# Three small edits to an eight-core attention and feed-forward kernel: the matmuls at its start go, a ring of product buffers gets a fourth slot, a pair of hidden-layer buffers becomes one

## The chip, the cores and the metric

The kernel runs on the 8 cores of one Trainium2 chip (two dies of four cores). Every core works on its own two sequences of the batch of 16 and never talks to the others. The metric is the device time in microseconds of the slowest core. PE is TensorE, DVE is VectorE, ACT is ScalarE, POOL is GpSimd, SP is SyncE, which here issues the loads of x and the stores of y.

## The reference

One pre-norm transformer layer on x of 16 x 2048 x 1024 in f32:

```python
x = x + attn(layernorm(x), W_qkv, b_qkv, W_proj, b_proj)     # 16 heads of 64
x = x + ffn(layernorm(x), Win, bin_, W1, b1, W2, b2, Wout, bout)

# attn: softmax(q k^T / 8) v with a "Fenwick" mask: token i sees itself, i-1, i-2, i-4, ... i-1024
#       and those few j with i on the Fenwick path of j
# ffn:
s = einsum('btd,dm->btm', x, Win) + bin_          # 1024 -> 64
h = relu(s[..., None] * W1 + b1)                  # 64 x 16 hidden values a token
g = einsum('btmh,mh->btm', h, W2) + b2            # 64
out = einsum('btm,md->btd', g, Wout) + bout       # 64 -> 1024
```

## The kernel before

A core goes through 16 chunks of 256 tokens (CH), eight for each of its two sequences. Every instruction is emitted once in Python order into a queue for its engine (class `Prog`). An engine runs its queue strictly in that order, and an instruction waits for the semaphores that its `deps` name. So the order of emission sets what stands behind a waiting instruction.

At the start DVE clears buffers, POOL and SP issue the weight loads, and PE runs 256 matmuls on `ones32` (L273 to L276, recorded as L274), each 128 columns wide. Nothing reads what they write.

A chunk does its attention within its own 128-token blocks (scores L907 and L913 on PE, exponentials L920 on ACT, weighted values L837), the far keys (below), the projection (L981) and the second layer norm. Then it prepares the next chunk: q, k (L720) and v (L774, evacuated at L785), and at last the feed-forward stage of its own tokens, into which the far scores of the next chunk are woven.

The far scores are elementwise products. For each distance o of 256, 512 and 1024 that the next chunk reaches, and each of 8 blocks dc of channels, `build_sparse` makes one **step** (L594 to L631). Step number k forms q times shifted k in two halves of 64 partitions: the low half at L617, on POOL where dc is even and on DVE where it is odd; the high half at L619, always on DVE. Then one matmul (L623, called m(k) here) sums the product over channels. The products of step k lie in a ring slot. Slot 1 is the second half of `tmpsp`, the others are in `ebuf`. Before step k may write its slot, the matmul that read the slot last must be done (`ebuf_rd[es]`); with three slots that is m(k-3). A chunk whose successor is the first of a sequence, or that has none, weaves in no steps (chunks 7 and 15); two weave in 8 steps (0 and 8), four weave in 16 (1, 2, 9, 10) and eight weave in 24.

The feed-forward stage: `s_sTb` is made by L1041 and evacuated by ACT at L1044. The 1024 hidden values a token are done in 8 pieces, ic = 0 to 7. For piece ic, h(ic) is a matmul L1068 on PE; its relu e(ic) writes `hT`, on ACT for even ic (L1087) and on DVE for odd ic (L1091); g(ic) is a matmul L1099 on PE that reads `hT` and accumulates into one bank. Three h are emitted ahead, h(ic+3) reuses the bank that e(ic) has read. `hT` has two halves, so e(ic) waits for g(ic-2) (`hT_rd[hs]`). The order of emission:

```python
h(0); step; h(1); step; h(2); step          # L1073 to L1076
for ic in range(8):                         # L1078
    e(ic); h(ic+3) if ic+3 < 8; g(ic); step; step
gaugT (ACT, L1104); the steps that are left; exp of the far scores (L645),
their transposes (L661, L665); Wout matmuls (L1121); residual (L1127)
```

So PE meets h(ic+3) behind the two step matmuls of the round before, and DVE meets e(odd) behind the products of two rounds. The Wout matmuls stand on PE behind L661, and so behind the last step.

Of the kernel before, what the change touches and what calls it, by code (L numbers as in the profile page):

```python
# [7 lines left out]
BF16 = mybir.dt.bfloat16  # L8
# [167 lines left out]
def build_program(cfg):  # L176
    nc = bass.Bass("TRN2", target_bir_lowering=False)
    T, CH, BPC, C, H = cfg.T, cfg.CH, cfg.BPC, cfg.C, cfg.H
# [28 lines left out]
    sbt = lambda n, shp, dt: st.enter_context(nc.sbuf_tensor(n, shp, dt))  # L207
    pst = lambda n, shp, dt: st.enter_context(nc.psum_tensor(n, shp, dt))

    with st:  # L210
# [17 lines left out]
        ones32 = sbt("s_ones32", [32, 128], BF16)  # L228
# [10 lines left out]
        scb = sbt("s_scb", [16, NO * CH], F32)  # L239
        sct = sbt("s_sct", [128, TPC * NO * 16], BF16)  # L240
        tmpsp = sbt("s_tmpsp", [128, 2 * VA_W], BF16)
        ebuf = sbt("s_ebuf", [128, 2 * CH], BF16)
        oT = sbt("s_oT", [128, NDC * CH], BF16)
        sTb = sbt("s_sTb", [64, CH], BF16)
        gaugT = sbt("s_gaugT", [65, CH], BF16)
        hT = sbt("s_hT", [128, 2 * CH], BF16)
        stats = sbt("s_stats", [128, 16 * TPC], F32)
        recip16 = sbt("s_recip", [128, 16], F32)

# [14 lines left out]
        P = Prog()  # L264
# [4 lines left out]
        t_cst = [t_cexp, t_ceps, t_czer]  # L269
        t_o32a = P.emit("vector", lambda ec: ec.memset(ones32[:, :], 0.0))  # L270
        t_ones = P.emit("vector", lambda ec: ec.memset(ones32[0:1, :], 1.0), deps=[t_o32a])
        t_heat = t_ones
        for _hk in range(256):  # L273
            t_heat = P.emit("tensor", lambda ec: ec.matmul(  # L274
                psc[0][:, 0:128], ones32[0:32, 0:128], ones32[0:32, 0:128],
                start=True, stop=True), deps=[t_ones] if _hk == 0 else [])  # L276
        t_qz0 = P.emit("vector", lambda ec: ec.memset(qZ[:, :], 0.0))
        t_bvz = P.emit("vector", lambda ec: ec.memset(bv_row[:, :], 0.0))
        t_bpz = P.emit("vector", lambda ec: ec.memset(bproj_row[:, :], 0.0))
# [2 lines left out]
        for dc in range(NDC):  # L282
            for k in range(2):
# [3 lines left out]
                              deps=[t_bo0])  # L287
# [103 lines left out]
        xT_rd = [[], []]  # L391
        xln_rd = [[], []]
        xln_w = [[], []]
        ebuf_rd = [[], [], []]
        scr_rd = []
        tt1_rd = [[]]
        hT_rd = [[], []]
        pmask_rd = [[], [], [], []]
        praw_rd = [[], []]
        x_ring_free = [[], []]  # L400
# [170 lines left out]
        def build_sparse(c2, qz_done2, qkv_done2):  # L571
            t0s = c2 * CH
            tile0s = t0s // 128
            sct_ready2 = {}
            steps = []
            valid_big = [(oi, o) for oi, o in enumerate(BIG) if t0s + CH > o]
            if not valid_big:
                return steps, None, sct_ready2
            per_bank = max(512 // CH, 1)
            nbank = (len(valid_big) + per_bank - 1) // per_bank  # L580
            sc_banks = [SPB[k] for k in range(nbank)]
            st_cell = {"war": None, "final": None}

            def get_war():
                if st_cell["war"] is None:
                    w = []
                    for bk in sc_banks:
                        w += psc_readers[bk]
                    st_cell["war"] = w
                return st_cell["war"]  # L590

            ei_cell = [0]
            for vi, (oi, o) in enumerate(valid_big):
                scp = rotb[sc_banks[vi // per_bank]]  # L594
                col0 = (vi % per_bank) * CH
                a = max(0, o - t0s)
                w = CH - a
                for dc in range(NDC):
                    def step(vi=vi, oi=oi, o=o, dc=dc, scp=scp, col0=col0, a=a, w=w):
                        es = ei_cell[0] % 3  # L600
                        ei_cell[0] += 1
                        kap_lo = kT[0:64, dc * T + t0s + a - o: dc * T + t0s + a - o + w]
                        kap_hi = kT[64:128, dc * T + t0s + a - o: dc * T + t0s + a - o + w]
                        qlo = qZ[0:64, dc * CH + a: dc * CH + a + w]
                        qhi = qZ[64:128, NDC * CH + dc * CH + a: NDC * CH + dc * CH + a + w]
                        if es != 1:
                            e0 = (es // 2) * CH
                            elo = ebuf[0:64, e0 + a:e0 + a + w]
                            ehi = ebuf[64:128, e0 + a:e0 + a + w]
                            e_in = ebuf[:, e0 + a:e0 + a + w]  # L610
                        else:
                            elo = tmpsp[0:64, VA_W + a: VA_W + a + w]
                            ehi = tmpsp[64:128, VA_W + a: VA_W + a + w]
                            e_in = tmpsp[:, VA_W + a: VA_W + a + w]
                        dq = qz_done2.get(dc, qkv_done2)
                        lo_eng = "gpsimd" if dc % 2 == 0 else "vector"
                        t_e1 = P.emit(lo_eng, lambda ec, elo=elo, qlo=qlo, kap_lo=kap_lo: ec.tensor_mul(  # L617
                            elo, qlo, kap_lo), deps=dq + ebuf_rd[es] + (scr_rd if es == 1 else []))
                        t_e2 = P.emit("vector", lambda ec, ehi=ehi, qhi=qhi, kap_hi=kap_hi: ec.tensor_mul(  # L619
                            ehi, qhi, kap_hi), deps=dq + ebuf_rd[es] + (scr_rd if es == 1 else []))  # L620
                        boap = bo[:, dc * 16:(dc + 1) * 16]
                        out_ap = scp[0:16, col0 + a: col0 + a + w]
                        t_mm = P.emit("tensor", lambda ec, out_ap=out_ap, boap=boap, e_in=e_in, dc=dc: ec.matmul(  # L623
                            out_ap, boap, e_in, start=(dc == 0), stop=(dc == NDC - 1)),
                            deps=([t_e1, t_e2, t_bo] + get_war()) if dc == 0 else [t_e1, t_e2])
                        ebuf_rd[es] = [t_mm]
                        st_cell["final"] = t_mm
                        for jt in range((t0s + a - o) // 128, (t0s + a - o + w + 127) // 128):
                            kv_rd[jt].append(t_e1)
                            kv_rd[jt].append(t_e2)  # L630
                        qT_rd.append(t_e1)  # L631
                        qT_rd.append(t_e2)
                    steps.append(step)

            def finish():
                nonlocal scb_rd, sct_rd
                t_exp_by_oi = {}
                for vi, (oi, o) in enumerate(valid_big):
                    scp = rotb[sc_banks[vi // per_bank]]
                    col0 = (vi % per_bank) * CH  # L640
                    a = max(0, o - t0s)
                    w = CH - a
                    in_ap = scp[0:16, col0 + a: col0 + a + w]
                    out_ap = scb[0:16, oi * CH + a: oi * CH + a + w]
                    t_exp = P.emit("scalar", lambda ec, in_ap=in_ap, out_ap=out_ap: ec.activation(  # L645
                        out_ap, in_ap, AF.Exp, bias=-8.0, scale=0.125),
                        deps=[st_cell["final"]] + t_cst + scb_rd)
                    t_exp_by_oi[oi] = t_exp
                for bk in sc_banks:
                    psc_readers[bk] = list(t_exp_by_oi.values())  # L650
                for i in range(TPC):
                    qg = tile0s + i
                    for oi, o in valid_big:
                        if qg * 128 < o:
                            continue
                        bank = rot6_next()
                        dst = rotb[bank]
                        src_ap = scb[0:16, oi * CH + i * 128: oi * CH + (i + 1) * 128]
                        out_ap = sct[:, (i * NO + oi) * 16:(i * NO + oi) * 16 + 16]
                        idap = identf[0:16, 0:16]  # L660
                        t_tr = P.emit("tensor", lambda ec, dst=dst, src_ap=src_ap, idap=idap: ec.transpose(  # L661
                            dst[:, 0:16], src_ap, idap),
                            deps=[t_exp_by_oi[oi], t_identf] + psc_readers[bank])
                        scb_rd = [t_tr]
                        t_ev = P.emit("vector", lambda ec, dst=dst, out_ap=out_ap: ec.tensor_copy(  # L665
                            out_ap, dst[:, 0:16]), deps=[t_tr] + sct_rd)
                        psc_readers[bank] = [t_ev]
                        sct_ready2[(i, oi)] = t_ev

            return steps, finish, sct_ready2  # L670
# [17 lines left out]
        for idx, (b, c) in enumerate(sched):  # L688
# [391 lines left out]
            for ic in range(8):  # L1080
                bank = h_banks[ic]
                scp = rotb[bank]
                hs = ic % 2
                bap = b1col[:, ic:ic + 1]
                hout = hT[:, hs * CH:(hs + 1) * CH]
                if ic % 2 == 0:
                    t_hev = P.emit("scalar", lambda ec, hout=hout, scp=scp, bap=bap: ec.activation(  # L1087
                        hout, scp[:, 0:CH], AF.Relu, bias=bap, scale=1.0),
# [6 lines left out]
                if ic + NHB < 8:  # L1095
                    sTb_rd = [emit_hmm(ic + NHB, [t_hev], bank=bank)]
                lhs2 = w2exp[:, ic * 64:(ic + 1) * 64]
                hin = hT[:, hs * CH:(hs + 1) * CH]
                t_g_last = P.emit("tensor", lambda ec, pbG=pbG, lhs2=lhs2, hin=hin, ic=ic: ec.matmul(  # L1099
                    pbG[0:64, 0:CH], lhs2, hin, start=(ic == 0), stop=(ic == 7)),  # L1100
                    deps=[t_hev] + (pbr_get(biG) if ic == 0 else []))
# [121 lines left out]
```

How the kernel before makes its waits and increments, by code:

```python
    def replay(self, eng, ec, sems):  # L155
        for fn, waits, key, inc in self.q[eng]:
            for (sk, sv) in waits:
                ec.wait_ge(sems[sk], sv)
            if fn is not None:
                instr = fn(ec)
                if key is not None:
                    instr.then_inc(sems[key], inc)
```

## Time and profile before

| | us |
|---|---|
| two timed runs | 1405.37 and 1471.52 (median 1438.44) |
| the profiled execution | 1403.41 |
| its span, slowest core (core 5) | 1401.8 |
| spans of the eight cores | 1394.8 to 1401.8 |
| busy on that core: PE, DVE, ACT, POOL | 1124.6, 764.9, 402.0, 186.8 |

The span runs from the first to the last instruction of a core, and 1.6 us of the profiled execution lie around it. Times in the rows are microseconds from the start of the span. A row of the timeline gives start, duration, engine, line, operation, tiles and count (rows of one kind are merged), and in brackets how long the engine had stood idle before it and what released it. A PE row's duration includes the drain of the last matmul, so a matmul's duration is longer than the distance to the next one.

### The profile page before, as it was taken

The numbers are of one execution on the slowest core, as the hardware profiler recorded it, in microseconds if no ns is written. First come the engines' busy times: TensorE is split into PE (matmuls) and PEld (weight loads), VectorE is DVE, ScalarE is ACT, GpSimd is POOL, SyncE is SP. The second block draws the span as 40 slices with busy tenths as digits, with TensorE's granted clock in tenths as the row PEclk, the third lists the DMA queues.
The fourth block names the chain that finished last, engine by engine and source line by source line (L and its number), as shares of the span: only waits on it lengthen the run. The fifth ranks groups of instructions, "written<-read, shape, count | busy, mean of one in ns | idle before, by whom it ended". The sixth has DMA issues, their size and how long they took to land.

```text
span 1401.8 us, 22118 instructions; the slowest of 8 cores (1394.8 to 1401.8 us)
## 1 busy us (share of the span) xinstructions
PE 1124.6 (80%) x6912; PEld 643.5 (46%) x6912; DVE 764.9 (55%) x2080; ACT 402.0 (29%) x899; POOL 186.8 (13%) x193
## 2 busy tenths in 40 slices
PE   7078888898888877888888788888787887987885
PEld 7054545453534535335354544445353443534542
DVE  6055535546574565745654545555556565565654
ACT  0114132423313233132332424132422314223221
POOL 1000101102021030210300010100103012031130
PEclk9999889898978969789798989889897887878976
DMA  9900010101001010010101010010101001010000
GB/s 146 167 1 1 1 61 1 61 1 61 1 14 48 1 61 1 1 61 1 61 1 61 1 44 18 1 61 1 61 1 51 11 1 61 1 48 13 1 31 30
DMA packets 13279, 43.82 MB, mean 31 GB/s; under 512 B 2608, under 2 KB 2864, under 8 KB 13168
## 3 DMA queue, kind: packets, MB, share of 16 engines
q1 hardware_dynamic: 9584, 33.65, 6.9%
q0 software_dynamic: 3584, 8.76, 4.1%
q8 instruction: 61, 1.00, 0.3%
q14 instruction: 50, 0.41, 0.1%
HBM read 34.38 MB, written 16.78 MB: 36 GB/s over the span
## 4 chain that ended last, share of the span: by engine, by line
PE 57%; DVE 15%; issue 13%; ACT 6%; another core or an unknown queue 3%; DMA 2%; POOL 1%; DVEq 1%; POOLq 0%; ACTq 0%; SPq 0%
PE p_o L720 7%; PE p_o L774 6%; PE p_A L981 6%; PE p_A L720 4%; PE p_B L981 4%; PE p_o L494 3%; PE p_o L623 3%; PE p_B L720 3%; ACT s_pmask L920 2%; PE p_B L774 2%; PE p_sc L907 2%; DVE s_xT L502 2%; PE p_sc L913 2%; PE p_o L939 2%
## 5 line engine op out<-in xcount | busy, mean ns | idle before, releaser
L617 POOL TENSOR_TENSOR s_ebuf<-s_qZ,s_kT 64x256 bf16<-64x256 bf16 x94 | 63.2, 673 | 593.8 <-DVE s_qZ L731 542.6
L720 PE MATMUL p_o<-s_xT,s_wqkv 128*128 128x256 bf16 x1152 | 133.7, 273 | 0.0
L920 ACT ACTIVATE s_pmask<-p_sc 128x512 bf16<-128x512 f32 (+1 forms) x192 | 103.9, 591 | 86.4 <-PE p_sc L913 85.1
L720 PEld LDWEIGHTS p_o<-s_xT,s_wqkv 128*128 128x128 bf16 x1152 | 112.8, 98 | 13.2
L437 ACT ACTIVATE s_xln<-s_x 128x1024 f32<-128x1024 f32 x32 | 33.5, 1049 | 245.4 <-DVE s_stats L434 245.4
L981 PE MATMUL p_A<-s_wproj,s_oT 128*128 128x512 bf16 x256 | 89.5, 513 | 11.7 <-DVE s_oT L502 11.2
L720 PE MATMUL p_A<-s_xT,s_wqkv 128*128 128x256 bf16 x512 | 69.3, 274 | 34.2 <-DVE s_qZ L731 20.3
L494 PE MATMUL p_o<-s_identf,s_xln 128*128 128x128 f32 x376 | 76.6, 303 | 20.5 <-DVE s_recip L953 16.5
L837 PE MATMUL p_o<-s_vaug,s_pmask 128*128 128x66 bf16 x992 | 70.1, 196 | 28.5 <-ACT s_pmask L920 27.4
L774 PE MATMUL p_o<-s_wqkv,s_xT 128*128 128x512 bf16 x384 | 91.2, 380 | 0.0
L837 PEld LDWEIGHTS p_o<-s_vaug,s_pmask 128*128 128x128 bf16 x992 | 58.2, 100 | 62.2 <-issue 42.2
L907 PE MATMUL p_sc<-s_qZ,s_kT 128*128 128x256 bf16 x372 | 85.0, 314 | 0.0
L913 PE MATMUL p_sc<-s_mb,s_ident 128*128 128x512 bf16 (+1 forms) x192 | 83.6, 436 | 0.0
L623 PE MATMUL p_o<-s_ebuf,s_bo 128*16 128x256 bf16 x182 | 59.4, 346 | 18.7 <-DVE s_ebuf L619 18.0
L992 DVE SCALAR_TENSOR_TENSOR s_x<-p_A,s_x 128x512 f32<-128x512 f32 x32 | 22.1, 692 | 95.4 <-PE p_A L985 95.4
L866 POOL TENSOR_TENSOR s_tmpsp<-s_vaug,s_sct 128x1056 bf16<-128x1056 bf16 x28 | 54.6, 1949 | 138.7 <-DVE s_sct L665 56.1
L494 PE MATMUL p_sc<-s_identf,s_xln 128*128 128x128 f32 x131 | 32.2, 301 | 49.8 <-DVE s_stats L547 48.1
L617 POOL TENSOR_TENSOR s_tmpsp<-s_qZ,s_kT 64x256 bf16<-64x256 bf16 x42 | 27.9, 665 | 329.4 <-PE p_o L623 328.3
L785 DVE CAST s_vaug<-p_o 128x512 bf16<-128x512 f32 x48 | 33.3, 694 | 69.9 <-PE p_o L778 69.9
L720 PEld LDWEIGHTS p_A<-s_xT,s_wqkv 128*128 128x128 bf16 x512 | 48.1, 98 | 49.6 <-issue 44.2
L494 PEld LDWEIGHTS p_o<-s_identf,s_xln 128*128 128x128 f32 x376 | 49.5, 153 | 36.4 <-issue 35.6
L619 DVE TENSOR_TENSOR s_ebuf<-s_qZ,s_kT 64x256 bf16<-64x256 bf16 x182 | 64.5, 369 | 1.6 <-PE p_o L623 0.2
(153 smaller groups left out, 2013.7 us busy)
## 6 DMA issues: line engine op xcount, KB each, us to landing
s_x<-x SPq DMA_DIRECT2D x16, 1024.0 KB, 5.3
y<-s_x SPq DMA_DIRECT2D x16, 1024.0 KB, 4.4
s_wqkv<-wqkv POOLq DMA_DIRECT2D x1, 6144.0 KB, 50.9
s_wproj<-wproj POOLq DMA_DIRECT2D x1, 2048.0 KB, 61.6
s_win<-win POOLq DMA_DIRECT2D x1, 128.0 KB, 61.5
s_woutaug<-wout POOLq DMA_DIRECT2D x1, 128.0 KB, 57.0
s_identf<-ident SPq DMA_DIRECT2D x1, 64.0 KB, 1.8
s_mb<-mb01x POOLq DMA_DIRECT2D x1, 64.0 KB, 57.0
```

The costliest lines, as they stand in the source:

```text
L494: t_tr = P.emit("tensor", lambda ec, dst=dst, si=si, src_ap=src_ap: ec.transpose(dst[:, si * 128:(si + 1) * 128], src_ap, identf[:, :]), d ...
L617: t_e1 = P.emit(lo_eng, lambda ec, elo=elo, qlo=qlo, kap_lo=kap_lo: ec.tensor_mul(elo, qlo, kap_lo), deps=dq + ebuf_rd[es] + (scr_rd if es ...
L619: t_e2 = P.emit("vector", lambda ec, ehi=ehi, qhi=qhi, kap_hi=kap_hi: ec.tensor_mul(ehi, qhi, kap_hi), deps=dq + ebuf_rd[es] + (scr_rd if ...
L623: t_mm = P.emit("tensor", lambda ec, out_ap=out_ap, boap=boap, e_in=e_in, dc=dc: ec.matmul(out_ap, boap, e_in, start=(dc == 0), stop=(dc = ...
L720: t_mm = P.emit("tensor", lambda ec, pb=pb, lhs=lhs, rhs=rhs, dc=dc: ec.matmul(pb[:, 0:CH], lhs, rhs, start=(dc == 0), stop=(dc == NDC - 1 ...
L774: t_mm = P.emit("tensor", lambda ec, pb=pb, lhs=lhs, rhs=rhs, dc=dc: ec.matmul(pb[:, 0:512], lhs, rhs, start=(dc == 0), stop=False), deps= ...
L837: t_pv = P.emit("tensor", lambda ec, out_ap=out_ap, lhs=lhs, rhs=rhs, st=st, stp=stp: ec.matmul(out_ap, lhs, rhs, start=st, stop=stp), dep ...
L866: t_ttA = P.emit("gpsimd", lambda ec, tout=tout, vin=vin, prep=prep: ec.tensor_mul(tout, vin, prep), deps=[sct_ready[(i, oi)], t_va1] + tt ...
L907: t_last = P.emit("tensor", lambda ec, out_ap=out_ap, lhs=lhs, rhs=rhs, first=first: ec.matmul(out_ap, lhs, rhs, start=first, stop=False), ...
L913: t_last = P.emit("tensor", lambda ec, scp=scp, width2=width2, mrep=mrep: ec.matmul(scp[:, 0:width2], ident[:, :], mrep, start=False, stop ...
L920: t_exp = P.emit("scalar", lambda ec, pm=pm, scp=scp, width2=width2: ec.activation(pm, scp[:, 0:width2], AF.Exp, bias=-8.0, scale=0.125), ...
L981: t_mm = P.emit("tensor", lambda ec, pb=pb, lhs=lhs, rhs=rhs, dc=dc: ec.matmul(pb[:, 0:512], lhs, rhs, start=(dc == 0), stop=False), deps= ...
```

## The change

The 256 matmuls at the start are not emitted. The ring of the steps has four slots: slot 1 is still in `tmpsp`, slots 0, 2 and 3 are in `ebuf`, which grows from 512 to 768 columns. `hT` shrinks from 512 to 256 columns and all eight pieces use it.

```diff
-        ebuf = sbt("s_ebuf", [128, 2 * CH], BF16)
+        ebuf = sbt("s_ebuf", [128, 3 * CH], BF16)
-        hT = sbt("s_hT", [128, 2 * CH], BF16)
+        hT = sbt("s_hT", [128, CH], BF16)
...
-        t_heat = t_ones
-        for _hk in range(256):
-            t_heat = P.emit("tensor", lambda ec: ec.matmul(
-                psc[0][:, 0:128], ones32[0:32, 0:128], ones32[0:32, 0:128],
-                start=True, stop=True), deps=[t_ones] if _hk == 0 else [])
...
-        ebuf_rd = [[], [], []]
+        ebuf_rd = [[], [], [], []]
-        hT_rd = [[], []]
+        hT_rd = [[]]
...
-                        es = ei_cell[0] % 3
+                        es = ei_cell[0] % 4
...
-                            e0 = (es // 2) * CH
+                            e0 = (0, None, CH, 2 * CH)[es]
...
-                hs = ic % 2
+                hs = 0
-                hout = hT[:, hs * CH:(hs + 1) * CH]
+                hout = hT[:, 0:CH]
...
-                hin = hT[:, hs * CH:(hs + 1) * CH]
+                hin = hT[:, 0:CH]
```

Step k now waits for m(k-4), and e(ic) waits for g(ic-1).

## Rows read from the trace of the kernel before

**Rows 1.** The chain that ended last, share of the span by engine.
```profile
PE 57%; DVE 15%; issue 13%; ACT 6%; another core or an unknown queue 3%; DMA 2%; POOL 1%; DVEq 1%; POOLq 0%; ACTq 0%; SPq 0%
```

**Rows 2.** Timeline of the start: start, duration, engine, line, what, idle before.
```profile
1.88 27.46 PE L274 MATMUL p_sc<-s_ones 32*128 32x128 bf16 x256 [1.88 <-DVE s_ones L271]
...
68.54 0.23 DVE L331 TENSOR_SCALAR s_w1exp<-s_ident,s_w1dup 64x64 bf16<-64x64 bf16 x1 [39.17 <-DMA s_ident<-ident]
...
77.43 0.45 PE L494 MATMUL p_sc<-s_identf,s_xln 128*128 128x128 f32 x1 [48.09 <-DVE s_stats L547]
...
82.53 1.86 PE L720 MATMUL p_A<-s_xT,s_wqkv 128*128 128x256 bf16 x8 [0.78 <-DVE s_xT L502]
...
88.63 1.04 PE L720 MATMUL p_A<-s_xT,s_wqkv 128*128 128x256 bf16 x8
```

**Rows 3.** Who waited for g: total us, times (the first also its longest).
```profile
ACT s_hT L1087 <- PE p_B L1099: 85.4, 48, 2.6
...
  DVE s_hT L1091: 8.8, 10
```

**Rows 4.** Timeline of chunk 7's feed-forward stage, which has no steps: its ACT instructions.
```profile
750.51 0.47 ACT L1087 ACTIVATE s_hT<-p_sc,s_b1col 128x256 bf16<-128x256 f32 x1 [0.51 <-PE p_sc L1068]
...
751.72 0.47 ACT L1087 ACTIVATE s_hT<-p_o,s_b1col 128x256 bf16<-128x256 f32 x1 [0.73 <-PE p_B L1099]
...
753.15 0.47 ACT L1087 ACTIVATE s_hT<-p_A,s_b1col 128x256 bf16<-128x256 f32 x1 [0.96 <-PE p_B L1099]
...
754.59 0.47 ACT L1087 ACTIVATE s_hT<-p_sc,s_b1col 128x256 bf16<-128x256 f32 x1 [0.96 <-PE p_B L1099]
...
756.09 0.47 ACT L1104 ACTIVATE s_gaugT<-p_B,s_b2col 64x256 bf16<-64x256 f32 x1 [1.03 <-PE p_B L1099]
```

**Rows 5.** Timeline of chunk 15's stage without steps: e(0), e(7) and gaugT.
```profile
1387.82 0.47 ACT L1087 ACTIVATE s_hT<-p_sc,s_b1col 128x256 bf16<-128x256 f32 x1 [0.51 <-PE p_sc L1068]
...
1392.08 0.48 DVE L1091 TENSOR_SCALAR s_hT<-p_A,s_b1col 128x256 bf16<-128x256 f32 x1 [0.65 <-PE p_B L1099]
...
1393.20 0.47 ACT L1104 ACTIVATE s_gaugT<-p_B,s_b2col 64x256 bf16<-64x256 f32 x1 [1.05 <-PE p_B L1099]
```

**Rows 6.** Timeline of the stages with 8 steps, chunks 0 and 8: e(4), gaugT; e(3), e(4).
```profile
167.23 0.47 ACT L1087 ACTIVATE s_hT<-p_A,s_b1col 128x256 bf16<-128x256 f32 x1 [2.07 <-PE p_B L1099]
...
170.39 0.47 ACT L1104 ACTIVATE s_gaugT<-p_B,s_b2col 64x256 bf16<-64x256 f32 x1 [1.17 <-PE p_B L1099]
...
824.46 0.48 DVE L1091 TENSOR_SCALAR s_hT<-p_sc,s_b1col 128x256 bf16<-128x256 f32 x1
...
825.16 0.47 ACT L1087 ACTIVATE s_hT<-p_A,s_b1col 128x256 bf16<-128x256 f32 x1 [2.44 <-PE p_B L1099]
```

**Rows 7.** Busy time by engine in chunk 14's stage with 24 steps (window, length, busy).
```profile
1322.40:1338.00 15.60, 11.69 (x39) 3.65 (x39) 14.23 (x36) 2.36 (x5) 6.69 (x10) 0.59 0.00 0
```

**Rows 8.** Line L617 alone: duration ns min, median, max on DVE.
```profile
L617 DVE TENSOR_TENSOR s_ebuf<-s_qZ,s_kT x88: 282/285/766, 163.4 to 1336.9; 64x256 bf16<-64x256 bf16 x88
```

**Rows 9.** Timeline of the same stage with 24 steps, chunk 14.
```profile
1326.03 0.68 POOL L617 TENSOR_TENSOR s_ebuf<-s_qZ,s_kT 64x256 bf16<-64x256 bf16 x1 [1.11 <-PE p_o L623]
...
1326.11 0.76 DVE L619 TENSOR_TENSOR s_ebuf<-s_qZ,s_kT 64x256 bf16<-64x256 bf16 x1
...
1326.89 0.47 ACT L1087 ACTIVATE s_hT<-p_A,s_b1col 128x256 bf16<-128x256 f32 x1 [2.41 <-PE p_B L1099]
1326.90 0.48 DVE L1091 TENSOR_SCALAR s_hT<-p_sc,s_b1col 128x256 bf16<-128x256 f32 x1
...
1329.90 0.48 DVE L1091 TENSOR_SCALAR s_hT<-p_o,s_b1col 128x256 bf16<-128x256 f32 x1
...
1332.89 0.48 DVE L1091 TENSOR_SCALAR s_hT<-p_A,s_b1col 128x256 bf16<-128x256 f32 x1
1332.91 0.66 POOL L617 TENSOR_TENSOR s_ebuf<-s_qZ,s_kT 64x256 bf16<-64x256 bf16 x1 [0.21 <-PE p_o L623]
```

**Rows 10.** Line L623, who waited for it: us, times.
```profile
  DVE s_ebuf L617: 5.8, 14
```

## The prediction

> **What bounds the kernel now.** I read the chain that ended last first: 57% of it is PE and 15% DVE [rows 1]. That is a mean over stages with different limits, so each edit has to be priced in its own stage. I went on to the timeline of the start (for the 256 matmuls), to the feed-forward stages of chunks 0, 7, 8, 14 and 15 (for `hT` and the ring), and to the lists of who waited for g and for m.
>
> At the start PE works from 1.88 to 29.3 us and then stands still for 48.09 us. DVE's wait at 68.54 ends with a weight load [rows 2]. The loads set the start, not PE.
>
> In a feed-forward stage without steps, PE, ACT and DVE pass one piece of data around and mostly wait. With 16 or 24 steps it is different: DVE is busy for 14.23 of 15.60 us [rows 7]. There DVE sets the pace, and ACT's 85.4 us of waiting for g [rows 3] cost nothing.
>
> **The 256 matmuls go: 0 us.** 27.46 us of PE work lie wholly under the loads, and PE then waits 48.09 us for data. The cover is the loads; if they were gone, the work would be worth up to 27 us. What could be lost is a warm PE. But when PE starts again it is slow with the matmuls in place: 8 of 256 columns in 1.86 us, against 1.04 us for the same 8 six microseconds later [rows 2], though the granted clock of the record is 1.00 in both. The first is the pace of 1.2 GHz, the second of 2.4 GHz. So the warmth is lost before, and I take 0. If it did last, the loss would be about 0.8 us on each of the first two or three groups of 8 and on the transposes ahead of them: 3 us, the upper bound. Below zero a gain of up to 1 us, should the loads land a little earlier.
>
> The Trainium skill (TensorE: Matmul & The Clock Gate, "What's actually happening") says that the array's clock is at half rate by default and that recent activity releases it. Taken alone this speaks for keeping the matmuls. The same section lets the clock fall back after idling, and the trace agrees: after 48.09 us the pace is the slow one.
>
> **One `hT` instead of two, stages without steps (chunks 7 and 15).** Now e(ic) may start when g(ic-2) is done, and e on ACT and e on DVE overlap. Afterwards e(ic), h(ic+3), g(ic), e(ic+1) is one serial chain. Its links can be read off. From e(0) to e(2), which waited for g(0), pass 751.72 - 750.51 = 1.21 us with PE at full pace. From e(4) to e(6), which waited for g(4), pass 754.59 - 753.15 = 1.44 us with PE slow [rows 4]. From e(7) to gaugT, with no h between, pass 1393.20 - 1392.08 = 1.12 us [rows 5]. The serial stage of chunk 7 is one link of 1.21, four of 1.44, three of 1.12: 10.33 us, against 756.09 - 750.51 = 5.58 us. That is +4.75 us. Chunk 15 has two links of 1.21 and three of 1.44: 10.10 against 5.38 us, +4.7. Nothing lies beside these stages, since PE has no other work in its queue until gaugT is there. Sum +9.5 us. Were every link with h 1.21 and every one without 1.0, it would be +7.2 (lower bound).
>
> **The same in the stages with 8 steps (chunks 0 and 8).** The steps last until round 2. e(3), now on DVE in order, has to wait for g(2), whose end is when e(4) starts now: 167.23 [rows 6]. From there the chain is e(3)-e(4) 1.21, e(4)-e(5) 1.44, then three links of 1.12 to gaugT after e(5), e(6), e(7): 167.23 + 6.01 = 173.2, against 170.39. That is +2.9 us. Chunk 8 shows the same: e(3) moves from 824.46 to 825.16, and its slow PE makes the rest like it. Sum +5.8 us, lower bound 5.
>
> **The ring's fourth slot, and `hT`, in the stages with 24 steps (eight chunks).** Two things meet here.
> First, while a POOL product runs, a DVE product stands: the one at 1326.11 takes 0.76 us beside the POOL one of 1326.03 [rows 9], where the median is 0.285 [rows 8]. That is a loss of 0.48 us for each such meeting, and there are up to ten in a stage. A relu from PSUM is not held: e(7) at 1332.89 takes its 0.48 us with POOL at work from 1332.91 [rows 9].
> Second, the single `hT` makes e(3) wait for g(2). In this stage g(2) ends just when DVE gets there: e(4) starts at 1326.89 and e(3) at 1326.90 [rows 9]. So e(3) is not late. What is queued behind a waiting e(odd) on DVE are the products of the next steps, and PE's m and h behind them.
> With four slots POOL's product k goes after m(k-4), one step earlier, so it no longer falls on the products ahead of e(3) but into DVE's wait for g, or under the relu. From e(3) to e(5) the serial chain wants 2 x 1.44 = 2.88 us, now it is 3.00: -0.1. From e(5) to e(7) there is no h: the chain wants 2.24, DVE wants 0.40 (the relu up to the next start) + 6 products of 0.285 + one meeting of 0.48 = 2.6, now it is 2.99: -0.4. Of the five steps after e(7) I give the ring 0.2 (between 0 and one meeting, 0.48). Together -0.7 us a stage, -5.6 us for eight.
> At the other end: four meetings gone and no wait for g, -1.9 a stage. Or e(3), e(5) and e(7) each late by the 0.70 us that chunk 8 shows (825.16 - 824.46), +2.1 a stage. I take a value near the first case, because chunk 14's own rows have g(2) in time.
> The direct wait of DVE for a slot is 5.8 us in 14 stages [rows 10], 0.4 each at the stage's start. It gives nothing: e(1) has to wait for g(0), which PE reaches no earlier.
>
> The Trainium skill (SBUF — State Buffer, "Who interferes with whom") says that whichever of DVE and GpSimd takes the shared port pair first holds it for its whole instruction. A GpSimd product could then also be the one that is held, which these rows don't show: POOL's took 0.66 to 0.68 us. By that rule a meeting moves its cost to POOL, and the sum changes only within its bounds.
>
> **Stages with 16 steps (four chunks).** The same pattern, but the last step is over before e(7), and gaugT sets the end. e(7) comes a little earlier by the ring, later by g(6): -0.15 each, -0.6 in all, bounds -0.4 and +0.6 each.
>
> **Sum.** 0 + 9.5 + 5.8 - 5.6 - 0.6 = +9.1 us, on the profiled execution's 1403.41: 1412.5 us. That execution agrees with the lower of the two timed runs, 1405.37. The stated median, 1438.44, is the mean of that and a run of 1471.52, and the forecast is for executions like the first.
>
> **Rivals.**
> *A, the ring wins more.* POOL's lead hides four meetings a stage: 8 x -1.9 and 4 x -0.4 give -16.8, with +15.3 for the other stages about -1.5: 1402 us. For it: DVE's share of these stages. Against: the serial chain floors them at 1.44 us a piece, near today's 1.50.
> *B, slower than before.* The wait for g takes DVE's time in the long stages. It is one mechanism: h(ic+3) and g(ic) stand on PE behind the step matmuls, these wait for DVE's products, and DVE waits for g. By 0.70 us at each of three odd pieces in 12 stages it adds 25 us instead of -6.2: 1403.4 + 15.3 + 25.2 = 1444 us. At a third of that, 0.25 us a piece, it is +24 in all, 1428. From 0.35 us a piece on, the kernel is slower by over 2%. For it: in chunk 8 e(3) comes 0.70 us ahead of g(2)'s end. Against: chunk 14, where they coincide.
> *C, the early matmuls mattered.* The slow start gets longer, by 3 us: 1415.5. Against: the slow 1.86 us after them. By the skill's rule on the clock gate alone, this would be the way.
>
> **How the numbers follow.** About 2% (28 us) is what a measurement of this kernel can tell from no change. Forecast (1405 to 1420 us): 0.6. A (1399 to 1405): 0.17. B (1420 to 1444): 0.18, of which 0.08 above 1431. C: 0.05. Faster by over 2% needs terms below every bound here: 0.02. Within 2%: 0.90. Slower: 0.08. Range 1401 to 1430, which leaves 0.1 at either end.
>
> **What would show each step.** The start: PE's first real matmul near 77.4 us, the first 8 of L720 in about 1.86 us. Chunks 7 and 15: e(0) to gaugT in 10 us, eight relus at 1.1 to 1.45 us from each other, ACT and DVE never at once. Chunks 0 and 8: about 10 us instead of 7.2. Chunk 14: e(3) to e(5) in 2.9 us, waits of DVE for L1099 of up to 0.5 us, POOL's products under them. It would be wrong if the odd relus of the long stages came over 3.1 us apart, or if time moved in a stage that no edit touches.

## The result and the profile after

| | before | after |
|---|---|---|
| timed runs, median | 1406.56 us (10 runs) | 1417.04 us (11 runs) |
| profiled execution | 1403.41 us | 1415.08 us |
| its span, slowest core | 1401.8 us | 1413.5 us |

The ratio of after to before is 1.0069, 95% interval 1.0055 to 1.0083: 9.7 us slower, within 2%. Either kernel now and then has a run some per cent longer, with a lower granted clock; the ratios leave such runs out, the medians of this table hold them, and the first median of before, 1438.44 us from two runs, was half made of one.

First the head of the page of the kernel after. Its lines stand 5 below those of before (L1087 is now L1082, L1091 is L1086, L1099 is L1094).

```profile
span 1413.5 us, 21497 instructions; the slowest of 8 cores (1409.2 to 1413.5 us)
...
PE 1083.2 (77%) x6608; PEld 615.8 (44%) x6656; DVE 744.4 (53%) x2080; ACT 401.8 (28%) x899; POOL 186.7 (13%) x193
...
PE 58%; DVE 17%; issue 13%; ACT 6%; another core or an unknown queue 3%; DMA 1%; POOL 1%; DVEq 1%; POOLq 0%; ACTq 0%; SPq 0%
```

PE does less (the matmuls at the start are gone) and DVE less (it stands fewer times behind POOL, as the count at the end of the experiments shows), and yet the span is longer. DVE has grown on the chain, from 15% [rows 1] to 17%. The waits for g (engine and line, released by; us, times, longest) say where:

```profile
ACT s_hT L1082 <- PE p_B L1094: 111.9, 48, 2.7
DVE s_hT L1086 <- PE p_B L1094: 49.8, 64, 3.5
```

DVE waited 8.8 us in 10 places for g [rows 3]; now it waits 49.8 us, at every odd relu.

Chunk 7's feed-forward stage, timeline of the kernel after, the relus and gaugT (start, duration, engine, line, what, idle before):

```profile
749.75 0.47 ACT L1082 ACTIVATE s_hT<-p_sc,s_b1col 128x256 bf16<-128x256 f32 x1 [0.51 <-PE p_sc L1063]
...
752.31 0.47 ACT L1082 ACTIVATE s_hT<-p_o,s_b1col 128x256 bf16<-128x256 f32 x1 [2.10 <-PE p_B L1094]
...
753.76 0.48 DVE L1086 TENSOR_SCALAR s_hT<-p_sc,s_b1col 128x256 bf16<-128x256 f32 x1 [2.31 <-PE p_B L1094]
...
755.21 0.47 ACT L1082 ACTIVATE s_hT<-p_A,s_b1col 128x256 bf16<-128x256 f32 x1 [2.42 <-PE p_B L1094]
...
756.65 0.48 DVE L1086 TENSOR_SCALAR s_hT<-p_o,s_b1col 128x256 bf16<-128x256 f32 x1 [2.41 <-PE p_B L1094]
...
757.77 0.47 ACT L1082 ACTIVATE s_hT<-p_sc,s_b1col 128x256 bf16<-128x256 f32 x1 [2.09 <-PE p_B L1094]
...
758.89 0.48 DVE L1086 TENSOR_SCALAR s_hT<-p_A,s_b1col 128x256 bf16<-128x256 f32 x1 [1.75 <-PE p_B L1094]
...
760.01 0.47 ACT L1099 ACTIVATE s_gaugT<-p_B,s_b2col 64x256 bf16<-64x256 f32 x1 [1.77 <-PE p_B L1094]
```

ACT and DVE take turns. From e(2) on, 1.45, 1.45, 1.44, 1.12 and 1.12 us pass from one relu to the next, and 1.12 from e(7) to gaugT. From e(0) to gaugT the stage takes 760.01 - 749.75 = 10.26 us, where it took 5.58 [rows 4].

Chunk 14's stage with 24 steps, DVE's relus e(1), e(3), e(5), e(7) and two of POOL's products between them:

```profile
1331.51 0.48 DVE L1086 TENSOR_SCALAR s_hT<-p_A,s_b1col 128x256 bf16<-128x256 f32 x1 [0.37 <-PE p_B L1094]
...
1334.51 0.48 DVE L1086 TENSOR_SCALAR s_hT<-p_sc,s_b1col 128x256 bf16<-128x256 f32 x1 [0.51 <-PE p_B L1094]
...
1337.41 0.48 DVE L1086 TENSOR_SCALAR s_hT<-p_o,s_b1col 128x256 bf16<-128x256 f32 x1 [0.51 <-PE p_B L1094]
...
1340.03 0.48 DVE L1086 TENSOR_SCALAR s_hT<-p_A,s_b1col 128x256 bf16<-128x256 f32 x1 [0.21 <-PE p_B L1094]
```
```profile
1333.87 0.66 POOL L612 TENSOR_TENSOR s_ebuf<-s_qZ,s_kT 64x256 bf16<-64x256 bf16 x1 [1.34 <-PE p_o L618]
1335.07 0.66 POOL L612 TENSOR_TENSOR s_ebuf<-s_qZ,s_kT 64x256 bf16<-64x256 bf16 x1 [0.54 <-PE p_o L618]
```

POOL's product of 1333.87 lies under DVE's idle time from 1334.00 to 1334.51 and the relu behind it, and costs DVE nothing; the one of 1335.07 still meets a product. The odd relus are 3.00, 2.90 and 2.62 us apart. Before, e(1) of this stage was

```profile
1324.04 0.48 DVE L1091 TENSOR_SCALAR s_hT<-p_A,s_b1col 128x256 bf16<-128x256 f32 x1
```

and the distances were 2.86, 3.00 and 2.99 us [rows 9]. DVE now idles 0.51 us before e(3) and e(5): the fourth slot has freed its time, and the single `hT` makes it wait that time out. From e(1) to e(3) the stage even gets longer.

**Where the time went.** For each of the 16 feed-forward stages I took the length from the start of L1044 (`s_sTb`) to the first residual addition (L1127 before) on the slowest core of each profile. The table gives the change against before in us, two chunks by themselves and the longer stages as sums; the runs in it follow below.

| kernel | chunks 7, 15 (no steps) | chunks 0, 8 (8 steps) | 16 steps, sum of 4 | 24 steps, sum of 8 | all stages | time, by the ratio |
|---|---|---|---|---|---|---|
| forecast | +4.75, +4.7 | +2.9, +2.9 | -0.6 | -5.6 | +9.1 | |
| **after** | +4.68, +4.84 | +3.46, +2.57 | -0.9 | -5.4 | **+9.2** | +9.7 |
| single `hT` alone | +4.77, +4.78 | +3.48, +3.00 | +1.4 | +0.3 | +17.7 | +19.4 |
| ring of four, two h buffers | 0.00, +0.12 | -0.77, -1.11 | -7.2 | -12.8 | -21.8 | -19.7 |
| ring of four, eight h buffers | -0.90, -1.50 | -1.04, -2.21 | -7.0 | -12.9 | -25.6 | -25.9 |
| ring of ten, two h buffers | -0.11, +0.08 | -0.39, -0.94 | -8.4 | -22.1 | -31.9 | -32.6 |
| ring of eight, five h buffers | -1.55, -1.20 | -2.34, -2.69 | -8.2 | -19.1 | -35.1 | -35.6 |
| DVE products, ring of three | +0.03, +0.12 | +0.23, +0.18 | -0.7 | +0.7 | +0.6 | -4.2 |
| DVE products, ring of four, two h | +0.10, +0.11 | +0.64, +0.17 | -0.7 | +1.0 | +1.2 | -0.8 |

Chunk 14's stage in its parts, us, from the relus' starts in the timelines:

| kernel | L1044 to e(1) | e(1) to e(3) | e(3) to e(5) | e(5) to e(7) | e(7) to the first L1127 | stage |
|---|---|---|---|---|---|---|
| before | 2.53 | 2.86 | 3.00 | 2.99 | 7.91 | 19.28 |
| after | 2.50 | 3.00 | 2.90 | 2.62 | 7.55 | 18.57 |
| ring of four, two h buffers | 2.16 | 2.57 | 2.39 | 2.86 | 7.63 | 17.61 |

Outside these stages a single chunk moves by up to 3 us either way from one profile to the next, in stretches that no edit touches. The last two columns differ by up to 2 us (5 us for the first kernel with DVE products), and I have no cause for that beyond this scatter.

### The profile page after: what moved, and what is told of

It reads as the page before. It is cut to its first block, busy times and chain, and to the rows that moved or that the text cites. A ratio compares the mean times of both kernels' runs of the same rounds, so it can differ in the third digit from the quotient of the medians.

```text
span 1413.5 us, 21497 instructions; the slowest of 8 cores (1409.2 to 1413.5 us)
## 1 busy us (share of the span) xinstructions
PE 1083.2 (77%) x6608; PEld 615.8 (44%) x6656; DVE 744.4 (53%) x2080; ACT 401.8 (28%) x899; POOL 186.7 (13%) x193
## 4 chain that ended last, share of the span: by engine, by line
PE 58%; DVE 17%; issue 13%; ACT 6%; another core or an unknown queue 3%; DMA 1%; POOL 1%; DVEq 1%; POOLq 0%; ACTq 0%; SPq 0%
PE p_o L715 7%; PE p_o L769 6%; PE p_A L976 5%; PE p_B L976 4%; PE p_A L715 4%; PE p_o L489 3%; PE p_o L618 3%; PE p_B L715 3%; ACT s_pmask L915 2%; PE p_B L1094 2%; PE p_sc L902 2%; DVE s_oT L497 2%; DVE s_xT L497 2%; PE p_B L769 2%
## 5 line engine op out<-in xcount | busy, mean ns | idle before, releaser
L612 POOL TENSOR_TENSOR s_ebuf<-s_qZ,s_kT 64x256 bf16<-64x256 bf16 x136 | 91.0, 669 | 917.1 <-DVE s_qZ L726 547.2
L715 PEld LDWEIGHTS p_o<-s_xT,s_wqkv 128*128 128x128 bf16 x1152 | 113.2, 98 | 13.5
L432 ACT ACTIVATE s_xln<-s_x 128x1024 f32<-128x1024 f32 x32 | 33.5, 1049 | 244.7 <-DVE s_stats L429 244.7
L976 PE MATMUL p_A<-s_wproj,s_oT 128*128 128x512 bf16 x224 | 79.2, 513 | 20.9 <-DVE s_oT L497 20.9
L987 DVE SCALAR_TENSOR_TENSOR s_x<-p_A,s_x 128x512 f32<-128x512 f32 x32 | 22.1, 692 | 95.8 <-PE p_A L980 95.8
L489 PEld LDWEIGHTS p_o<-s_identf,s_xln 128*128 128x128 f32 x376 | 49.8, 153 | 36.4 <-issue 35.6
L1039 ACT ACTIVATE s_sTb<-p_A,s_bincol 64x256 bf16<-64x256 f32 x16 | 7.5, 468 | 198.3 <-PE p_A L1036 198.3
L976 PE MATMUL p_B<-s_wproj,s_oT 128*128 128x512 bf16 x256 | 61.9, 385 | 0.0
## 6 DMA issues: line engine op xcount, KB each, us to landing
s_wqkv<-wqkv POOLq DMA_DIRECT2D x1, 6144.0 KB, 49.8
```

The source lines that it names most:

```text
L489: t_tr = P.emit("tensor", lambda ec, dst=dst, si=si, src_ap=src_ap: ec.transpose(dst[:, si * 128:(si + 1) * 128], src_ap, identf[:, :]), d ...
L715: t_mm = P.emit("tensor", lambda ec, pb=pb, lhs=lhs, rhs=rhs, dc=dc: ec.matmul(pb[:, 0:CH], lhs, rhs, start=(dc == 0), stop=(dc == NDC - 1 ...
L976: t_mm = P.emit("tensor", lambda ec, pb=pb, lhs=lhs, rhs=rhs, dc=dc: ec.matmul(pb[:, 0:512], lhs, rhs, start=(dc == 0), stop=False), deps= ...
```

## The experiments

**The single `hT` alone.** On the kernel before:

```diff
-        hT = sbt("s_hT", [128, 2 * CH], BF16)
+        hT = sbt("s_hT", [128, CH], BF16)
-                hs = ic % 2
+                hs = 0
```

> Kernel before with the single hT alone: the 256 matmuls and the ring of three stay. My theory (the serial chain of relu, h and g costs where few steps are woven in, DVE sets the pace elsewhere): chunks 7 and 15 +4.7 us each, chunks 0 and 8 +2.9 each, the four stages with 16 steps +0.3 each, those with 24 steps 0: +16 to +17 us in all. Rival (DVE also loses its time to the wait for g in the long stages): 0.7 to 2.1 us more in each of 12 stages, +24 us or more in all.

Measured: ratio 1.0138 (1.0125 to 1.0152), +19.4 us, a little above the 16 to 17 expected; the stages sum to +17.7, and 16.0 of them lie in chunks 0, 7, 8 and 15. Those with 24 steps hardly move (between -0.10 and +0.25 us each). So the wait for g takes nothing from DVE there as long as the ring has three slots: rival B falls for this kernel. What is left is the serial chain of the short stages.

**The start without its matmuls.** The loop of 256 goes, nothing else.

> Kernel before without the 256 matmuls at the start, nothing else. My theory: they lie under the weight loads and their warmth is gone after 48 us, so 0 us, and the first 8 matmuls of the q projection still take about 1.86 us. Rival (they kept something warm): +3 us, with a start that is slow for longer.

Measured: ratio 1.0005 (0.9996 to 1.0015), so between 0.6 us faster and 2.1 us slower. No effect is seen, and the rival's 3 us are excluded. PE's first work and the first projection, timeline:

```profile
75.78 0.45 PE L489 MATMUL p_sc<-s_identf,s_xln 128*128 128x128 f32 x1 [75.78 <-DVE s_stats L542]
...
80.88 1.87 PE L715 MATMUL p_A<-s_xT,s_wqkv 128*128 128x256 bf16 x8 [0.79 <-DVE s_xT L497]
```

The pace of the first projection is that of before, 1.86 us [rows 2].

**More of the same matmuls, up to the data.** `range(256)` becomes `range(680)`.

> Kernel before with 680 matmuls at the start in place of 256: at 107 ns each they end near 75 us, just ahead of the first transposes at 77.4. If idleness is what makes PE slow at the first projection, its first 8 matmuls take about 1.04 us in place of 1.86, and the kernel is 2 to 3 us faster. If the pace there has another cause, nothing moves.

Measured: ratio 1.0028 (1.0009 to 1.0047), not faster but 1 to 7 us slower, for which I have no cause.

```profile
59.75 14.81 PE L274 MATMUL p_sc<-s_ones 32*128 32x128 bf16 x137
77.78 0.45 PE L494 MATMUL p_sc<-s_identf,s_xln 128*128 128x128 f32 x1 [3.22 <-DVE s_stats L547]
...
82.88 1.87 PE L720 MATMUL p_A<-s_xT,s_wqkv 128*128 128x256 bf16 x8 [0.79 <-DVE s_xT L502]
```

The last 137 take 14.81 us, 108 ns each, after 58 us of nothing else. 128 columns in 107 ns are 1.2 columns a nanosecond, the pace of 1.2 GHz. It is not the price of a weight load for each matmul: in the kernel before, four matmuls of 66 columns, each with a weight load of its own, take 0.28 us together, the drain included:

```profile
119.91 0.28 PE L837 MATMUL p_o<-s_vaug,s_pmask 128*128 128x66 bf16 x4 [0.98 <-ACT s_pmask L920]
```

These matmuls never ran at PE's fast pace, in this kernel or in the one before (27.46 us for 256 is 107 ns as well, [rows 2]). My reason in the prediction, that their warmth is lost in the 48 us of idleness, was wrong: there was none to lose. The rule of the Trainium skill that I weighed there (TensorE: Matmul & The Clock Gate, "What's actually happening"), that recent activity releases the clock, did not help either: the trace disagrees with it for these matmuls, 72 us of which released nothing, and the trace decides.

**Large matmuls up to the data.**

```diff
+        t_hot = P.emit("vector", lambda ec: ec.memset(kT[:, 0:640], 1.0))
-        for _hk in range(256):
-                psc[0][:, 0:128], ones32[0:32, 0:128], ones32[0:32, 0:128],
+        for _hk in range(330):
+                psc[0][:, 0:512], kT[:, 0:128], kT[:, 128:640],
```

> Kernel before with 330 matmuls of 128 rows and 512 columns on ones at the start, in place of 256 of 32 rows and 128 columns. The 680 small ones ran at 107 ns each to 74.6 us and left the first projection as slow as ever (1.87 us for 8). Theory: their size or shape never brought PE to its fast pace. Then the large ones go over to about 0.21 us each, end near 72 to 75 us and the first projection takes nearer 1.04 us: 2 to 3 us faster. Rival (three us of idleness before the first transposes are enough to slow PE again, or f32 transposes keep it slow): the first projection stays at 1.87 us.

The first row is the start of the second one, cut off at 6.2 us:

```profile
2.55 3.93 PE L274 MATMUL p_sc<-s_kT 128*128 128x512 bf16 x9 [2.55 <-DVE s_kT L272]
2.55 73.21 PE L274 MATMUL p_sc<-s_kT 128*128 128x512 bf16 x324 [2.55 <-DVE s_kT L272]
75.94 0.30 PE L494 MATMUL p_sc<-s_identf,s_xln 128*128 128x128 f32 x1 [0.17 <-DVE s_stats L547]
...
80.22 1.03 PE L720 MATMUL p_A<-s_xT,s_wqkv 128*128 128x256 bf16 x8 [1.58 <-DVE s_xT L502]
```

The first nine still come 0.43 us apart, 1.2 columns a nanosecond. 512 columns in 0.22 us (73.21 us for 330; a few records are missing) are the fast pace, nearly 2.4 columns a nanosecond. PE goes over to the transposes after 0.17 us, and the first projection runs at 1.03 us. So PE can be had warm at the data. The time shows no gain: ratio 1.0003 (0.9983 to 1.0023). The interval excludes the 3 us that I had expected at most, not 2 us. In the mean of the eight cores chunk 0's feed-forward stage starts at 159.4 us in this profile, at 161.3 before and at 160.3 without the matmuls. That is 1 to 2 us, from one execution of each kernel; whether it is real, or given back later, stays open.

**The ring of four without the single `hT`.** So that no buffer grows, the odd pieces of the kernel after go to the first 256 columns of `oT`, which rests during the feed-forward stage:

```diff
-                hs = 0
+                hs = ic % 2
+                hbuf = hT[:, 0:CH] if hs == 0 else oT[:, (hs - 1) * CH:hs * CH]
...
+            oT_rd = mx(*(oT_rd + [t_g_last]))
```

> Changed kernel with the second hidden buffer given back: the odd pieces are written to the first 256 columns of oT, which nothing reads at that time. So this is the ring of four, without the single hT. If the gain of the long stages comes from the ring itself: chunks 7 and 15 back to 5.4 to 5.6 us, chunks 0 and 8 to 7.2 to 7.7, the long stages at least as short as in the changed kernel: 5 to 8 us faster than before. If the gain needed DVE's wait for g (POOL's products fall under it), the long stages return to their length of before, and the kernel is within 1 us of before.

Measured: ratio 0.986 (0.9847 to 0.9873), 19.7 us faster than before, far beyond the 5 to 8 expected; the rival (within 1 us of before) falls. Each stage with 24 steps loses 1.4 to 1.7 us, those with 16 steps 1.6 to 2.1. Chunk 14, DVE's four odd relus:

```profile
1307.44 0.48 DVE L1087 TENSOR_SCALAR s_oT<-p_A,s_b1col 128x256 bf16<-128x256 f32 x1
...
1310.01 0.48 DVE L1087 TENSOR_SCALAR s_oT<-p_sc,s_b1col 128x256 bf16<-128x256 f32 x1
...
1312.40 0.48 DVE L1087 TENSOR_SCALAR s_oT<-p_o,s_b1col 128x256 bf16<-128x256 f32 x1
...
1315.26 0.48 DVE L1087 TENSOR_SCALAR s_oT<-p_A,s_b1col 128x256 bf16<-128x256 f32 x1
```
```profile
1309.85 0.66 POOL L612 TENSOR_TENSOR s_ebuf<-s_qZ,s_kT 64x256 bf16<-64x256 bf16 x1 [1.05 <-PE p_o L618]
1311.05 0.67 POOL L612 TENSOR_TENSOR s_ebuf<-s_qZ,s_kT 64x256 bf16<-64x256 bf16 x1 [0.54 <-PE p_o L618]
```

They are 2.57, 2.39 and 2.86 us apart, and none waits for g. POOL's product of 1309.85 lies mostly under the relu of 1310.01, as I had thought it would, but now DVE goes on at once instead of waiting.

**All products on DVE.** On the kernel before:

```diff
-                        lo_eng = "gpsimd" if dc % 2 == 0 else "vector"
+                        lo_eng = "vector"
```

> Kernel before with all products of the steps on DVE; POOL makes none. Theory (a DVE product that meets a POOL product loses 0.48 us, more than the 0.25 us that the product costs DVE itself): the eight stages with 24 steps lose up to ten meetings (4.8 us) and gain ten products (2.5 us), so 1.5 to 2.3 us shorter each, those with 16 steps about 1: 14 to 22 us faster. Rival (POOL's help is worth its price, DVE is the bound and gets more work): 2.5 us longer in each long stage, 25 us slower.

Measured: ratio 0.997 (0.9951 to 0.9989), 4 us faster and not 14 to 22. Two odd relus of chunk 14:

```profile
1329.93 0.48 DVE L1091 TENSOR_SCALAR s_hT<-p_o,s_b1col 128x256 bf16<-128x256 f32 x1
...
1332.79 0.48 DVE L1091 TENSOR_SCALAR s_hT<-p_A,s_b1col 128x256 bf16<-128x256 f32 x1
```

These are 2.86 us apart, where the kernel before has 2.99. The products between them start as follows, first DVE's and POOL's of the kernel before, then the first three of this kernel:

```profile
1330.30 0.76 DVE L617 TENSOR_TENSOR s_tmpsp<-s_qZ,s_kT 64x256 bf16<-64x256 bf16 x1
1331.07 0.29 DVE L619 TENSOR_TENSOR s_tmpsp<-s_qZ,s_kT 64x256 bf16<-64x256 bf16 x1
1331.28 0.29 DVE L619 TENSOR_TENSOR s_ebuf<-s_qZ,s_kT 64x256 bf16<-64x256 bf16 x1
1331.59 0.28 DVE L617 TENSOR_TENSOR s_ebuf<-s_qZ,s_kT 64x256 bf16<-64x256 bf16 x1
1331.89 0.29 DVE L619 TENSOR_TENSOR s_ebuf<-s_qZ,s_kT 64x256 bf16<-64x256 bf16 x1
1332.10 0.75 DVE L619 TENSOR_TENSOR s_tmpsp<-s_qZ,s_kT 64x256 bf16<-64x256 bf16 x1
...
1330.25 0.66 POOL L617 TENSOR_TENSOR s_ebuf<-s_qZ,s_kT 64x256 bf16<-64x256 bf16 x1 [0.53 <-PE p_o L623]
1332.02 0.68 POOL L617 TENSOR_TENSOR s_tmpsp<-s_qZ,s_kT 64x256 bf16<-64x256 bf16 x1 [1.11 <-PE p_o L623]
```
```profile
1330.33 0.27 DVE L617 TENSOR_TENSOR s_tmpsp<-s_qZ,s_kT 64x256 bf16<-64x256 bf16 x1
1330.62 0.29 DVE L619 TENSOR_TENSOR s_tmpsp<-s_qZ,s_kT 64x256 bf16<-64x256 bf16 x1
1330.94 0.28 DVE L617 TENSOR_TENSOR s_ebuf<-s_qZ,s_kT 64x256 bf16<-64x256 bf16 x1
```

From one start to the next, undisturbed, pass 0.30 us from a low half to its high half and 0.31 to 0.32 from a high half to the next low half, but only 0.21 from a high half to the next high half, which follows where POOL makes the low half between. So a product that DVE makes in place of POOL costs it 0.30 + 0.32 - 0.21 = 0.41 us between two odd relus, not 0.25. A meeting costs 0.77 - 0.30 = 0.47 us, near the 0.48 of the prediction. Two products more and two meetings less make 2 x 0.41 - 2 x 0.47 = -0.12 us, against the measured 2.86 - 2.99 = -0.13. Over a whole stage it comes out even: 33.5 us of standing in the eight stages go, 96 more products come, and the stages are 0.7 us longer, DVE's idle time 1.2. So a product costs 0.34 us in the mean, and there are twelve more of them a stage where I had reckoned with ten. The feed-forward stages explain none of the 4 us, whose place I have not found.

**The ring of four, two h buffers and all products on DVE.** The edits of the last two together.

> Ring of four with two hidden buffers (the kernel that was 1.4% faster) and all products on DVE. If the ring's gain is that POOL's products fall less often on DVE's, it is used up once POOL makes none, and this kernel comes out like the one with three slots and DVE products, within 3 us. If the two gains have different causes, they add: another 10 us or more below the ring alone.

Measured: ratio 0.9994 (0.9974 to 1.0015). With POOL out of it the fourth slot is worth nothing: the stages are those of the ring of three with DVE products, +1.2 against +0.6 us in sum. So the ring's gain needs POOL's products: nothing of it is left when POOL makes none.

**The kernel after with all products on DVE.**

> The changed kernel (ring of four, single hT) with all products on DVE. In the changed kernel POOL's products fall under DVE's waits for g and its relus. DVE with 8 products of 0.30 us and a relu of 0.40 us between two odd pieces needs 2.8 us, and the chain of the single hT 2.9 us: so the odd relus stay 2.9 us apart and DVE's wait for g shrinks to about 0.1 us, where the changed kernel showed 0.5. The steps after e(7) get about 0.5 to 0.8 us longer, since POOL's help is gone. 3 to 8 us slower than the changed kernel, 13 to 18 us slower than the one before. Rival (POOL's products are still in DVE's way in the changed kernel): as fast as the changed kernel or faster.

Measured: ratio 1.0121 (1.0105 to 1.0136), 17 us slower than before, 7 us slower than the kernel after. I use only its time: as expected, and against the rival. In the kernel after, POOL's products are where they hurt little, and taking POOL away takes that back. How the 7 us lie in the stages is not shown.

**Eight h buffers.** The same as the two, with `ic % 8`: one in `hT`, seven in `oT`.

> Ring of four with eight hidden buffers (one in hT, seven in oT): no relu waits for a g. If the reuse of the hidden buffer is still part of the chain in stages without steps, chunks 7 and 15 fall from 5.5 to about 4.6 us, chunks 0 and 8 by 0.5 us, and the kernel is 2 to 5 us faster than with two buffers. If the reuse of the h banks or PE's pace sets the chain, nothing moves. The long stages are DVE's in either case: below 0.3 us each.

Measured: ratio 0.9816 (0.9778 to 0.9854), 25.9 us faster than before (20.5 to 31.2). Its interval overlaps that of two buffers (0.9847 to 0.9873), so the 6 us between the two are uncertain; the stages differ by 3.8, within the 2 to 5 expected. Chunks 7 and 15 fall by 0.9 and 1.5 us, those with 24 steps stay as they were with two buffers. So even two buffers held the stages without steps.

**A longer ring.** Six more slots in `oT`, two h buffers; and four more slots with five h buffers (`es % 10` and `es % 8`; a slot of `oT` also waits for its readers, `oT_rd`).

> Ring of ten slots (six more in oT, which nothing else uses between the projection and the next chunk's attention) and two hidden buffers (hT and the last eighth of oT). POOL idles 22 us ahead of each stage and can now make the products of steps 0, 2, 4, 6 and 8 there, before DVE starts on its own. If meetings with POOL are what DVE's pace consists of, the long stages get 1 to 1.5 us shorter than with four slots: 10 to 18 us below the ring of four with two hidden buffers. If PE or DVE's own 0.3 us a product sets the pace by now: below 5 us.

> Ring of eight slots and five hidden buffers (hT and four in oT). POOL makes four products ahead of the stage. Chunks 7 and 15 at 4.6 us or less as with eight hidden buffers (0.9 to 1.5 us shorter than with two), the long stages within 0.5 us of those with ten slots. In all 2 to 4 us faster than ten slots with two hidden buffers, if the lead of five products isn't needed; slower than that one if it is.

Measured: 0.9768 (0.9755 to 0.9781) and 0.9747 (0.9732 to 0.9762): 32.6 and 35.6 us faster than before. POOL's first products for one of the last chunks of the second kernel, timeline:

```profile
1267.69 1.47 POOL L617 TENSOR_TENSOR s_ebuf<-s_qZ,s_kT 64x256 bf16<-64x256 bf16 x2 [21.36 <-DVE s_qZ L731]
1269.31 0.66 POOL L617 TENSOR_TENSOR s_oT<-s_qZ,s_kT 64x256 bf16<-64x256 bf16 x1
1270.37 0.66 POOL L617 TENSOR_TENSOR s_oT<-s_qZ,s_kT 64x256 bf16<-64x256 bf16 x1 [0.40 <-DVE s_qZ L731]
1291.55 0.68 POOL L617 TENSOR_TENSOR s_ebuf<-s_qZ,s_kT 64x256 bf16<-64x256 bf16 x1 [20.52 <-PE p_o L623]
```

Four products are made 20 us ahead of the stage. Eight slots with five h buffers beat both kernels, at 1369.49 us (median of 6) beside 1405.10 before. Eight slots come 3 us below ten, as expected (2 to 4), by the short stages: there the five h buffers win 6.4 us over the two. In the long stages the shorter ring costs: ten slots take 2.5 to 3.0 us off each of those with 24 steps, eight take 2.2 to 2.5.

**The stages with 24 steps, counted.** For the eight of them on the slowest core I took DVE's products that lasted over 0.31 us (held by POOL), the time by which they exceeded the undisturbed 0.29, and the time in which DVE ran nothing, us:

| kernel | products held | time they stood | DVE idle | stages, change |
|---|---|---|---|---|
| before | 80 | 33.5 | 27.5 | |
| after | 48 | 20.0 | 36.0 | -5.4 |
| single `hT` alone | 79 | 32.6 | 28.7 | +0.3 |
| ring of four, two h | 64 | 24.0 | 24.7 | -12.8 |
| ring of eight, five h | 48 | 17.7 | 24.5 | -19.1 |
| ring of ten, two h | 41 | 14.2 | 25.1 | -22.1 |

The changes of the two middle columns add up to that of the stages within 0.5 us in every row; with all products on DVE none is held. The ring of four takes 9.5 us of standing away, and 2.8 of idle time, which lie at the stages' start: the wait for a slot [rows 10] goes, and L1044 to e(1) falls from 2.53 to 2.16 us. (With the single `hT` e(1) waits there for g(0) instead, as I had said.) In the kernel after, 13.5 us of standing go, but DVE idles 8.5 us more.

## Why the prediction was right or wrong

**The sum, and the step that failed.** The change was forecast at +9.1 us, the measured rise is 9.7 (7.7 to 11.7), and the stages alone give +9.2. The step that failed is the base, not a term. The prediction put its sum on the profiled execution's 1403.41 and let the stated 1438.44 stand beside it, the mean of two timed runs 66 us apart. Set against that figure, 1412.5 us reads like a gain of 1.8%, and the kernel became 0.7% slower. The runs put the kernel before at 1406.56, the median of ten: 31.9 us below the stated figure and 3.2 above the base. Of the 4.5 us by which 1417.04 exceeds 1412.5, those 3.2 come from the base. A number for the time is only as good as the run it is added to.

The chances that I gave add up to 1.02, and rival C's 1415.5 us lies inside the forecast's own 1405 to 1420.

**The stages without steps: right.** +4.75 and +4.7 forecast, +4.68 and +4.84 measured, and +4.77 and +4.78 by the single `hT` alone. The links 1.21, 1.44 and 1.12, read from gaps of before whose wait ended with the right g, came out in chunk 7 as 2.56 for the first two together, then 1.45 and 1.12. This worked because a chain that waits for one thing already shows its links.

**The stages with 8 steps: right in sum.** +5.8 forecast, +6.0 measured. In chunk 0 PE ran slowly earlier than I had it (h(4) took 0.37 us, where it took 0.27 before), +3.5; in chunk 8 it was +2.6. That the two misses cancel is luck.

**The matmuls at the start: right number, wrong reason.** No worth of them is seen (1.0005, interval 0.9996 to 1.0015), but not since their warmth was lost: they ran at the pace of 1.2 GHz throughout. Their own row says so, 27.46 us for 256 of 128 columns [rows 2]. I had read that row only for its length.

**The long stages: right sum, partly by luck.** I forecast -6.2 for the twelve, and -6.3 came out. But the ring alone gives -20.0 there and the single `hT` alone +1.7. The other 12.0 us are neither edit's: they arise where the two meet. My step had it in one sentence, that the serial chain wants 2.88 us between two odd relus. That floor is what the kernel after shows (2.90 from e(3) to e(5)), and the ring of four without it shows 2.39. Since I priced the two together against the floor, the sum held. Had they been priced one by one and added, it would have been -18.

Inside the stage errors cancel. From e(1) to e(3) I had no change; chunk 14 shows +0.14. From e(5) to e(7) I had 2.6 us of DVE's own work; 2.62 came out, but as 2.41 of work and 0.21 of waiting for g. Behind e(7) I had -0.2; it was -0.36. Of the forecast -0.7 a stage, -0.71 in chunk 14 is a better agreement than the parts deserve.

**Rival A** (the ring wins more) was right about the ring and wrong about the kernel: 1.9 us a stage was its price, 1.6 is what the ring alone takes off. Its four meetings a stage did go in the kernel after (ten held products became six), but the wait for g, which it had left out, took 1.1 us a stage. The floor that I named against it is what kept it away.

**Rival B** (DVE's time goes to the wait for g) did not happen: with a ring of three the stages with 24 steps stay within 0.25 us. With a ring of four DVE does wait, 0.51 us before e(3) and e(5), but it waits out time that the ring had given it.

**Rival C** falls with the start's ratio of 1.0005.

**The price of a meeting.** The 0.48 us, from one pair of rows, is the price of a full meeting; the mean of the 80 held products in the stages with 24 steps is 0.42, since some start late in POOL's. What made me expect 14 to 22 us from taking POOL away was the other side, DVE's products, twelve a stage at 0.34 us and not ten at 0.25. The Trainium skill (SBUF — State Buffer, "Who interferes with whom") has the rule that the first to start holds the shared port pair for its whole instruction. The rows agree for DVE standing behind POOL. Where DVE is first, POOL pays:

```profile
1236.44 0.29 DVE L619 TENSOR_TENSOR s_tmpsp<-s_qZ,s_kT 64x256 bf16<-64x256 bf16 x1
1236.47 0.78 POOL L617 TENSOR_TENSOR s_ebuf<-s_qZ,s_kT 64x256 bf16<-64x256 bf16 x1 [1.01 <-PE p_o L623]
1236.65 0.76 DVE L619 TENSOR_TENSOR s_ebuf<-s_qZ,s_kT 64x256 bf16<-64x256 bf16 x1
```

DVE's product is not held and POOL's takes 0.78 us in place of 0.66. But this spares DVE nothing here, since its next product stands behind POOL's all the same. The prediction had taken such a meeting to move its cost to POOL.

## What to carry to other kernels

An edit that frees an engine and an edit that adds a wait for it can't be priced one by one: find the floor that the new wait sets between two events, and price both against it. Here halving one small buffer to lengthen a ring turned 20 us of gain into 10 us of loss, and a buffer that rests in that stage (`oT`) had the room for both. And before using a row as proof that work warms or hides something, divide its time by its columns: the row itself says at which pace it ran.

## What the runs showed of the hardware

- 680 matmuls of 32 rows and 128 columns ran at 107 to 108 ns each for 72 us on end, the pace of 1.2 GHz, and with 3.22 us of idleness behind them left the next projection slow (1.87 us for 8). 330 matmuls of 128 rows and 512 columns went over from 0.43 to 0.22 us each, the pace of 2.4 GHz, and with 0.17 us of idleness left it fast (1.03 us). The granted clock in the record is 1.00 in both stretches.
- A DVE product that meets a POOL product loses up to 0.48 us, 0.42 in the mean of 80; a product that DVE makes itself, in place of POOL, costs 0.34 us in the mean, 0.41 between two odd relus. POOL's help is worth having only where its products fall under waits, or under relus from PSUM: with POOL out of the way altogether the kernel before runs 0.3% faster, and the ring of four with two h buffers 1.4% slower.
- Two DVE products of 0.29 us that follow each other start 0.30 to 0.32 us apart where low and high halves alternate, and 0.21 us apart where two high halves follow each other.
- With a ring long enough for POOL to start 20 us ahead of the stage, while it idles, the same help is worth more: from four slots to ten the held products fall from 64 to 41 in the stages with 24 steps, and these by another 9 us in sum. What of it the lead does and what the longer ring within the stage, no run separates.
